# Gathers of the two unweighted passes written out one by one, with fixed index columns

## The reference, cut to what matters

```python
def _general_conv(x, src, dst, W_msg, b_msg, W_self, b_self, n_nodes):
    msg = x[src] @ W_msg + b_msg
    agg = jax.ops.segment_sum(msg, dst, num_segments=n_nodes)
    return agg + x @ W_self + b_self
...
h = _general_conv(x, src, dst, W1_msg, b1_msg, W1_self, b1_self, n)
h = jax.nn.leaky_relu(h, negative_slope=0.1)
out = _general_conv(h, src, dst, W2_msg, b2_msg, W2_self, b2_self, n)
```

## Time and profile before

| what | us |
|---|---|
| median of 3 timed runs | 10801.46 (10778.44 to 10802.27) |
| profiled execution | 10752.12 |
| its span in the profile | 10750.4 |
| PE busy | 6331.9 (59%) |
| DVE busy | 5005.6 (47%) |
| ACT busy | 1331.9 (12%) |
| POOL busy | 5855.2 (54%) |

### The profile page before, as it was taken

The page is one execution under the profiler, slowest core; times in us unless marked ns, Lnnn a source line. Parts: engine busy times, 40 slices in busy tenths (PEclk is TensorE's granted clock), DMA queues, the critical chain, the costliest instruction groups (busy, mean ns, idle before and its releaser), DMA issues. The chain is left out here.

```text
span 10750.4 us, 137753 instructions
## 1 busy us (share of the span) xinstructions
PE 6331.9 (59%) x24674; PEld 4941.0 (46%) x24675; DVE 5005.6 (47%) x12212; ACT 1331.9 (12%) x3940; POOL 5855.2 (54%) x5805
## 2 busy tenths in 40 slices
PE   4888875757466666555554555555555642222575
PEld 2888864546344444433333444444444442222454
DVE  6555558885444444355553222242222321114888
ACT  2222211213222222100001000010000300000000
POOL 3777740000288888777775777747777167763000
PEclk9898878988777777676766777677777655555798
DMA  4666674541377777644433222222222166663454
GB/s 147 189 190 187 186 231 152 169 136 35 69 104 105 104 104 105 111 134 137 133 117 91 82 82 82 82 75 81 83 83 83 41 193 204 201 193 99 129 170 155
DMA packets 835068, 1358.92 MB, mean 126 GB/s; under 512 B 112279, under 2 KB 488661, under 8 KB 834981
## 3 DMA queue, kind: packets, MB, share of 16 engines
q0 software_dynamic: 315328, 634.04, 26.7%
q1 hardware_dynamic: 385684, 562.46, 16.0%
q10 hardware_dynamic: 133968, 161.50, 4.8%
HBM read 943.05 MB, written 414.50 MB: 126 GB/s over the span
## 5 line engine op out<-in xcount | busy, mean ns | idle before, releaser
L1012 POOL DMA_INDIRECT rows_in<-table,gather_rows x2352 | 2500.5, 1063 | 1034.2 <-issue 511.1
L1103 PE MATMUL ps_p<-rows_in,hot 128*128 x5280 | 2000.5, 542 | 1584.6 <-SPq L976 1328.8
L1103 PEld LDWEIGHTS ps_p<-rows_in,hot 128*128 128x128 f32 x5280 | 1360.3, 271 | 2180.1 <-issue 1928.7
L1722 POOL DMA_INDIRECT scatter_sums<-regionC,idx x880 | 1387.3, 1576 | 307.1 <-issue 246.0
L956 DVE TENSOR_TENSOR regionC<-regionC,ps_p 128x257 f32 (+2 forms) x1320 | 558.6, 423 | 1767.9 <-DVEq L953 1569.1
L1464 PE MATMUL ps_p<-regionA 128*128 128x265 f32 (+1 forms) x3520 | 969.4, 435 | 426.0 <-DVE regionC L956 194.4
L1464 PEld LDWEIGHTS ps_p<-regionA 128*128 128x128 f32 x3520 | 735.3, 214 | 659.8 <-DVE regionC L956 239.3
L1012 POOL DMA_INDIRECT regionB<-table,gather_rows x784 | 848.4, 1082 | 344.5 <-issue 272.2
L1012 POOL DMA_INDIRECT regionC<-table,gather_rows x784 | 817.1, 1042 | 296.7 <-issue 265.1
L1927 PE MATMUL psS<-dst_scores,regionA 128*128 x1760 | 393.4, 362 | 793.7 <-issue 385.4
L1927 PEld LDWEIGHTS psS<-dst_scores,regionA 128*128 128x128 f32 x1760 | 383.7, 330 | 803.4 <-issue 803.4
(11 more groups left out here) (303 smaller groups left out, 8011.7 us busy)
## 6 DMA issues: line engine op xcount, KB each, us to landing
regionA<-edge_rows SPq DMA_DIRECT2D x880, 256.0 KB, 3.2
edge_rows<-regionB SPq DMA_DIRECT2D x196, 512.0 KB
edge_rows<-regionC SPq DMA_DIRECT2D x392, 256.0 KB
regionC<-srcrow_d SPq DMA_DIRECT2D x220, 256.0 KB
scatter_sums<-zero_rows ACTq DMA_DIRECT2D x8, 6400.0 KB, 42.3
regionA<-scatter_sums ACTq DMA_DIRECT2D x49, 1024.0 KB
rows_in<-table,gather_rows POOLq DMA_INDIRECT x2352
regionB<-rrow_d ACTq DMA_DIRECT2D x110, 256.0 KB
```

What stands on the lines that cost most here:

```text
L1012: g.indirect_dma_start(out=rows_of(b * per + j), out_offset=None, in_=table, in_offset=bass.IndirectOffsetOnAxis(ap=rows[j], axis=0), boun ...
L1103: x = te.matmul(ps[(u.c * VG + j) % NB][:, 0:width], hot[:, b, 2 * j + k, :], at_tile(G, slot[j] * 2 + k), start=k == 0, stop=k == 1)
L1722: g.indirect_dma_start(out=scat, out_offset=bass.IndirectOffsetOnAxis(ap=idx[:, b, j:j + 1], axis=0), in_=sums[:, b, j, :], in_offset=None ...
```

## The change

A second helper, `gather_straight`, issues the 784 gathers without a loop. Since each gather's number is fixed when the program is written, it takes its index column straight from `gidx`. It waits for the ring's slot once in each group of four, as before. The unweighted passes use it, and have no `gather_rows`; the weighted pass and the two other phases keep `gather`.

```diff
+        def gather_straight(g, table, rows_of, s_rows, ring, per, free):
+            top_row = g.to_reg(NP - 1)
+            for k in range(ET):
+                b = k // per % ring
+                if k % per == 0:
+                    g.wait_ge(free[b], 1)
+                    g.sem_inc(free[b], -1)
+                g.indirect_dma_start(out=rows_of(k % (ring * per)), out_offset=None, in_=table, in_offset=bass.IndirectOffsetOnAxis(ap=gidx[:, k:k + 1], axis=0), bounds_check=top_row, oob_is_err=True).then_inc(s_rows[b].sem, 16)
+
...
-                idx = sb('gather_rows', [P, RG, EG], I32, ctx)
+                idx = sb('gather_rows', [P, RG, EG], I32, ctx) if weighted else None
...
-                        gather(g, table, lambda k: G[:, k, 0:D], s_rows, RG, EG, ring_free, idx)
+                        if weighted:
+                            gather(g, table, lambda k: G[:, k, 0:D], s_rows, RG, EG, ring_free, idx)
+                        else:
+                            gather_straight(g, table, lambda k: G[:, k, 0:D], s_rows, RG, EG, ring_free)
```

## The result

| what | us |
|---|---|
| changed kernel, median of 4 runs | 10664.52 (10659.3 to 10673.92) |
| kernel before, median of 4 runs | 10797.9 (10778.44 to 10802.27) |
| ratio | 0.9881, 95% interval 0.9864 to 0.9898 |
| span of the changed kernel's profile | 10657.6 |

What follows compares the result with a forecast made beforehand. GpSimd's stream was taken to bound both unweighted passes: 1035 us of gathers + 10 of long gaps + 50 of collisions = 1095 a pass against 1246. That is 302 us less in all, 10801.5 - 302 = 10499, range 10390 to 10640.

Steps and rivals of the forecast that it cites:

- The bound: Both unweighted passes run at the pace of GpSimd, one gather in 1.589 us; whatever leaves its stream leaves the span.
- The handoff and the copy: Between groups of four gathers, the gap of 1.00 us becomes 0.30; straight, a pass is 784 x 1.32 = 1035 us.
- rival B: At each group's first gather, the 0.79 us come from standing behind a wait and stay: 10699 us, chance 0.05.
- The long gap each 96 gathers: Within the passes, a 1.76 us gap instead of 0.30, seven times a pass, not tied to the copy: 10 us kept.
- Collisions: Gathers starting within one of VectorE's 110 one-hots a pass are late: 50 us a pass, bounds 0 and 121.
- rival D: In the straight gathers, GpSimd starves for instructions, new code that runs once: slower, 11071 us, chance 0.03.
- The ring slot, costed at nothing: The wait and decrement ahead of each group's first gather cost 0, since the slot is free and the sequencer runs ahead.
- rival C: In the two passes another bound takes over, TensorE with its waits or the landing: within 30 us of 10801, chance 0.04.

Runs made afterwards that it cites:

- c2: The changed kernel run again in the third set, with waited-on counts taken as max(count, 0): 10388.26 us, ratio 0.9697 to the kernel before.
- e1: The changed kernel's straight gathers with each group's copy of index columns and the wait for it put back: 10704.51 us, ratio 0.9998 to the kernel before.
- e2: The kernel before, loop and copies kept, but each group's copy of index columns issued two groups ahead: 10423.42 us, ratio 0.9739.
- e1b: The changed kernel with each group's copy and the wait for it put back, run once more in the third set: 10712.17 us, ratio 1.0.
- e3: The changed kernel with one more wait ahead of each group, for the landed rows of the group two before: 10383.32 us, ratio 0.9699.
- e4: The changed kernel with a GpSimd memset of 192 elements behind each gather, waited for only five gathers later: 10570.5 us, ratio 0.9876.
- e6b: The changed kernel with straight gathers in the weighted pass too, and a wait for rows of the group two before; second run: 10242.44 us, ratio 0.9567.
- e7: The changed kernel with a two-element memset behind each second gather and a wait for the memset before: 10391.16 us, ratio 0.9702; again, 10384.16 us, 0.9706.

## Why the prediction was wrong

Step by step, against the profile after and c2:

- *The bound* was right as long as the slots came in time: in c2 GpSimd's stream sets the pace of both passes, and what left it left the span. In the profile after it does so only between the stops.
- *The handoff and the copy*: right. Gathers follow each other at 0.30 us across groups too. e1 shows that without their removal there is no gain, which also settles rival B, and e2 splits them: 0.64 us a group for the wait, 0.06 for the copy.
- *The long gap each 96 gathers*: kept at 10 us a pass, and wrong. I had argued that it isn't tied to the copy, since it falls between two gathers of a group. But it goes with the wait for the copy. All seven are there in each pass whose stream waits for its own copy at once (the kernel before, every weighted pass in the loop, e1 and e1b), and none in any other pass of the sets without late steps, straight or looped (c2, e2, e3, e4, e6b, e7). In the profile after, three and one are left. Why, no run shows. Without these 10 us the sum is 1085 us, and c2's passes took 1082.5 and 1085.9.
- *Collisions*: gathers over 1.1 us add up to 41 and 42 us a pass in the profile after, 50 and 53 us in c2. Forecast 50. In c2's first pass no gather of over 1.1 us starts outside a one-hot, and the 87 gathers that ran already as one began took at most 1.02 us.
- *Straight code, rival D*: 0.9998 and 1.0 in e1 and e1b. By the Trainium skill ("Runtime: NRT & Kernel Launch", section "Instruction fetch mechanics") straight code is fetched ahead; these runs agree, with a cost of at most 0.1%.
- *The ring slot, costed at nothing*: this is the step that failed. Its argument was that rows land 3.3 us after a group's gathers and that TensorE has time to spare. TensorE's wait for landed rows did shrink, to 54.8 us. But the argument took the time of the handoff from TensorE to VectorE, and of a register step of SP, as the loop's rows had it. In the profile after, that handoff took over 4 us at least 40 times in the first pass, where a visit then takes 7 us instead of 2; the ring of six groups runs dry, with 26 and 29 stops of over 1 us ahead of a group, 105 and 110 us in all. In the first pass they exceed the usual gap by 97 us, and fewer long gaps and collisions take back some 15: that is the 81 us that the pass lies above the forecast. GpSimd's wait for a ring slot was the sign of rival C, to which I gave 0.04; it came by a mechanism that I had not named, and not at C's price, which was within 30 us of 10801.

Where there are no late steps the working holds but for the long gap: passes of 1082.5 and 1085.9 us against 1095 forecast, and a ratio of 0.9697 against 10499 / 10801.5 = 0.972. So whether the forecast was met hung on the set, which the prediction had no term for. The kernel before shows it too: it took 10797.9 us beside the result and 10763.9 in the second set, the two that have late steps, and 10701.3 to 10710.3 in the four that have none.

What stays open: why some sets have late steps and others none. It goes by no chip number: sets one, two and four ran on chips numbered 4, sets three and five on 0 and 14, and of these only the second had them; whether the 4 was the same chip each time isn't recorded. The neighbours' work wasn't varied, nor was the recording of the profile: that recording itself delays the steps isn't excluded. The profiled execution lies among or near the timed ones of its set, save for the kernel before of the result, whose profile (10752) lies under its timed runs (10778 to 10802), so late steps may differ from one execution to the next. Nor is it shown what in the change multiplies them in the two passes, the lead of six gathers, the missing wait, the pace or the straight code: the four kernels made to tell these apart (e1, e2, e4, e7) met only sets without them. In the sets that have late steps, the loop of this helper, with its wait of 1 us in each group, had 1 to 4 in a pass and the straight passes 55 to 91.

## What to carry to other kernels

When a wait on an engine's own small work is taken away (here some 160 us a pass: 1243 in e1, 1082.5 in c2), look at what else runs beside the denser stream. Before forecasting, read the register steps of the other queues in the trace of before, in every phase that has such a stream (here a median of 46 ns and a longest of 1521): they tell whether other queues suffer in that execution. And put the changed kernel itself into each set of experiments: without that control I took the set's effect for the gate's.

## What was not expected of the hardware

- The same program differs by 1.5% between sets in its ratio to the kernel before (0.985 and 0.9697), with intervals of 0.2% to either side. In the slower one register steps of other queues come late beside the gathers, most of them by 0.7 us, and the handoff from TensorE to VectorE by up to several us.
- The gap of 1.8 us in each 96 gathers isn't a property of the gathers: where there are no late steps it is there in every stream that waits for its own copy in each group at once, and in none that doesn't.
- A small memset between two gathers costs almost nothing: the gap ahead of the next gather shrinks from 0.30 to 0.19 us by a memset of 0.12.
- GpSimd's sequencer runs 6 gathers ahead of the one that runs, in straight code and in a loop alike, where nothing in the stream waits for GpSimd's work of just before, and a further wait on landed rows two groups back leaves that unchanged.
- In these passes a gather is held up only if it starts under a one-hot of VectorE, until some 0.12 us before its end; one that runs already isn't, nor is the one-hot.
